# Second attention with row maxima by four head pairs instead of eight, and half of the shared expert moved into the routing

## The reference, cut to what matters

```python
# attention b: 16 heads of 8, per sample 256 queries x 256 keys
attn = jnp.einsum('abhqd,abhkd->abhqk', q, k) * scale
attn = jax.nn.softmax(attn, axis=-1)
out  = jnp.einsum('abhqk,bhkd->abhqd', attn, v)
out  = jnp.swapaxes(out, 1, 2).reshape(B, N, D)      # then @ proj_w.T + proj_b
# ffn: 64 experts of width 64, 8 chosen per token out of 4 of 8 groups, and a shared expert of width 128
h       = jax.nn.silu(g) * u * coef[:, :, None]
moe_out = jnp.einsum('tei,eih->th', h, Wd)
shared  = jax.nn.silu(x @ SWg) * (x @ SWu) @ SWd
```

## Time and profile before

| | us |
|---|---|
| median of 3 runs | 1084.95 (1084.47 to 1090.1) |
| the profiled execution's own time | 1086.67 |
| its span | 1084.9 |
| second attention's loop, from DVE's first uninterrupted maxima to the last copy of its output | 645.1 to 777.7 |
| from there to the first matmul of the shared expert's second half | 777.7 to 808.0 |
| expert loop of the second FFN and the end | 808.0 to 1084.9 |

### The profile page before, as it was taken

How to read it: one execution, slowest core, us unless ns; L and a number is a source line. 1 busy time by engine, 2 the same in 40 slices (tenths; PEclk the granted TensorE clock), 3 DMA queues, 4 the chain that set the end, 5 groups by cost and what they waited for, 6 DMA issues and landing times. The chain is left out here.

```text
span 1084.9 us, 17540 instructions
## 1 busy us (share of the span) xinstructions
PE 971.3 (90%) x5387; PEld 694.7 (64%) x5387; DVE 959.2 (88%) x1447; ACT 671.2 (62%) x848; POOL 368.7 (34%) x266
## 2 busy tenths in 40 slices
PE   6767887878669999999999899899889999999997
PEld 4533444444347888888888555455568888888886
DVE  7799999999988999999999797987589999999997
ACT  4779999999934545445445554876544544545544
POOL 2054666667901433333331211111203333333330
PEclk9865555555669999999999998999789999999999
DMA  2000000000119555555550000112049555555521
GB/s 59 1 1 1 1 1 1 1 1 1 52 30 215 157 160 151 147 157 147 155 153 4 1 1 1 23 23 31 16 107 225 151 147 157 148 154 155 147 85 39
DMA packets 50711, 86.94 MB, mean 80 GB/s; under 512 B 20092, under 2 KB 33404, under 8 KB 50556
## 3 DMA queue, kind: packets, MB, share of 16 engines
q1 hardware_dynamic: 50664, 86.34, 30.6%
HBM read 83.33 MB, written 2.98 MB: 80 GB/s over the span
## 5 line engine op out<-in xcount | busy, mean ns | idle before, releaser
L1514 ACT ACTIVATE sg<-ps 128x512 f32<-128x512 f32 x264 | 156.8, 594 | 264.8 <-PE ps L523 263.2
L523 PE MATMUL ps<-xh,whi 128*128 128x512 f32 x528 | 206.2, 391 | 1.3 <-ACT b L1330 1.3
L523 PE MATMUL ps<-xl,whi 128*128 128x512 f32 x528 | 205.9, 390 | 0.0
L523 PE MATMUL ps<-xh,wlo 128*128 128x512 f32 x528 | 205.8, 390 | 0.0
L2329 DVE TENSOR_TENSOR hf<-sg,ps 128x512 f32<-128x512 f32 x264 | 170.3, 684 | 29.9 <-DVE hl L2336 24.4
L1727 POOL CAST whi<-wraw 128x384 fp32r<-128x384 f32 x66 | 66.3, 1004 | 370.2 <-PE ps L523 285.5
L1647 POOL TENSOR_TENSOR rr<-xr,rr 128x2048 f32<-128x2048 f32 x32 | 145.2, 4569 | 125.0 <-ACT rr L1305 71.2
L2336 DVE TENSOR_TENSOR hl<-hf,hh 128x1024 fp32r<-128x1024 f32 x132 | 178.2, 1350 | 0.8 <-DVE hf L2329 0.8
L2341 DVE TENSOR_TENSOR hf<-hf,cbc 128x1024 f32<-128x1024 f32 x128 | 157.6, 1231 | 13.4
L1542 ACT ACTIVATE hh<-hf 128x1024 fp32r<-128x1024 f32 x132 | 139.2, 1055 | 4.6 <-DVE hf L2341 4.6
L1729 POOL TENSOR_TENSOR wlo<-wraw,whi 128x384 fp32r<-128x384 f32 x66 | 116.3, 1762 | 5.3
(11 more groups left out here) (277 smaller groups left out, 1512.3 us busy)
## 6 DMA issues: line engine op xcount, KB each, us to landing
cbc<-routing_coefficients SPq DMA_DIRECT2D x256, 256.0 KB, 3.8
wraw<-in_wexp_dram SPq DMA_DIRECT2D x66, 192.0 KB, 2.7
X<-in_x_dram SPq DMA_DIRECT2D x4, 256.0 KB, 4.8
routing_coefficients<-cT SPq DMA_DIRECT2D x8, 128.0 KB, 2.3
out_dram<-X SPq DMA_DIRECT2D x4, 256.0 KB, 2.9
heads_by_row<-o_all SPq DMA_DIRECT2D x12, 72.0 KB
b_rows<-heads_by_row SPq DMA_DIRECT2D x12, 72.0 KB, 2.7
rope_in<-in_consts_dram SPq DMA_DIRECT2D x1, 512.0 KB, 3.4
```

The source lines that it names most:

```text
L523: return pe.matmul(o, l, r, start=start, stop=stop, **kw)
L1514: act.activation(sg[c % 2][:, :], bank(4 + 2 * (c % 2)), ACT.Silu).then_inc(s_sg, 1)
```

## The change

The maxima are handled in *quads* of four units (`QUAD = UNITS // 2`), 16 rounds instead of 8, each with half as many maxima; the distance AHEAD falls from 11 to 8. The round's steps on PE stand at V % 4 = 1 and 2 instead of V % 8 = 0, 1 and 2. The path's steps stand some units earlier. `copy_out`'s last pair but one gets bank 2 beside bank 6. In the steps without raw scores, extra matmuls are put in (`TAIL_FILL`). The transposed tokens of the second FFN's groups 0 to 2 are copied by ACT instead of DVE, those of group 3 by DVE. The sigmoids of half 0 are taken group by group. The routing of half 0 is spread between the steps of the last two quarters of the path. In `prepare_f(1)` the shared expert's chunks 2 and 3 come on PE directly behind chunks 0 and 1, ahead of the second half's coefficients; DVE multiplies gate and up of chunks 0 and 1 between `route_masks` and `route_experts`. No product is left out in either version.

```diff
-AHEAD = UNITS + 3
+QUAD = UNITS // 2
+AHEAD = QUAD + 4
...
+        def pair_bank(n):
+            return 2 if n == 2 * B - 2 else 6
...
-            WAITS_FOR_PATH = {39: 4, 46: 3, 47: 4, 55: 4, 62: 3, 63: 4}
+            WAITS_FOR_PATH = {36: 4, 41: 3, 42: 4, 52: 4, 57: 3, 58: 4}
+            TAIL_FILL = {56: 1, 57: 1, 58: 2, 59: 1, 60: 2, 61: 1, 62: 2, 63: 2, 64: 2, 65: 2, 66: 2}
...
             def b_max_step(V):
-                s, at = (V - UNITS) // UNITS, (V - UNITS) % UNITS
-                if V >= UNITS and at == 0:
-                    b_max_transposed(s)
-                elif V >= UNITS and at in (1, 2):
-                    b_max_selected(s, at - 1)
+                k, at = V // QUAD - 1, V % QUAD
+                if 0 <= k < 2 * B:
+                    if at == 1:
+                        b_max_transposed(k)
+                    elif at == 2:
+                        b_max_selected(k)
...
                 for V in range(2, AHEAD):
                     b_tiles(-1, V)
                     b_max_step(V)
-                    if V >= AHEAD - 3:
-                        keep_busy(3, 6)
+                    keep_busy(3, 3)
...
+                    if U in (56, 57):
+                        pe.wait_ge(s_mx, 2 * B * UNITS + U - 57)
+                        logits(1, 0, U - 56)
...
             def prepare_f(f):          # PE
                 for c in range(2):
                     gate_up((PAIRS + 1) * FF_STEPS * f + c, 3, c, True)
+                if f == 1:
+                    shared_second(f)   # gate_up for chunks 2 and 3
...
             def samples_b():           # POOL
-                for s in range(B):
-                    max_split(s)
-                    if s == 1:
+                for k in range(2 * B):
+                    max_split(k)
+                    if k == 3:
                         pool.wait_ge(s_q2, 4)
                         pool.tensor_tensor(xb, xb, pb_s[:, :].unsqueeze(1).broadcast_to([P, TILES, P]), ALU.add
                                            ).then_inc(s_pbx, 1)
...
             def prepare_f(f):          # DVE
                 if f == 1:
-                    route_experts(f, 0)
+                    lows(f, 1)
                 route_bests(f, 1)
                 route_groups(f, 1)
                 route_masks(f, 1)
+                if f == 1:
+                    shared(f, 0)
                 route_experts(f, 1)
-                lows(f, 1)
+                if f == 0:
+                    lows(f, 1)
```

More of the change, by code:

```diff
@@ L952, in pv_b @@
                 if C % 2 == 0 and half == 0 and C >= 2:
-                    pe.wait_ge(s_bev, C // 2)
-                last = pv(vt, s, c, wr[:, C % CHUNKS, :], bank(6)[:, C % 2 * N:(C % 2 + 1) * N], (half,))
+                    if pair_bank(C // 2) == 2:
+                        pe.wait_ge(s_mx, 2 * B * UNITS - 2)
+                    else:
+                        pe.wait_ge(s_bev, min(C // 2, 2 * B - 2))
+                last = pv(vt, s, c, wr[:, C % CHUNKS, :], bank(pair_bank(C // 2))[:, C % 2 * N:(C % 2 + 1) * N], (half,))
                 if half == MT - 1:
@@ L1091, in gate_up, with shared_second @@
                     last.then_inc(done, 1)
+            def shared_second(f):
+                pe.wait_ge(s_xl, FF_STEPS * (f + 1))
+                for c in range(2, FF_STEPS):
+                    gate_up((PAIRS + 1) * FF_STEPS * f + c, 3, c, False)
             def prepare_f(f):
@@ L1133, in y @@
                     last.then_inc(s_yd, 1)
-                pe.wait_ge(s_xl, FF_STEPS * (f + 1))
-                for c in range(2, FF_STEPS):
-                    gate_up(s0 + c, 3, c, False)
+                if f == 0:
+                    shared_second(f)
                 with pe.Fori(0, PAIRS // 4) as i:
@@ L1429, in samples_b, with copy_xT, logit_exps @@
                         f_norm_rstd(1, 2)
-            def logit_exps(f, i):
-                act.wait_ge(s_lg, lap(f, i, 1))
+            def copy_xT(g, n):
+                act.wait_ge(s_fxnT, GROUPS + g + 1)
+                act.activation(f_xT[g][:, :], bank(n), ACT.Copy).then_inc(s_fxT, 1)
+                act.wait_ge(s_fxT, GROUPS + g + 1)
+                f_high(g)
+            def logit_exps(f, i, groups=range(2)):
+                act.wait_ge(s_lg, lap(f, i, groups[-1]))
                 if f == 0:
                     act.wait_ge(s_S, CHUNKS * B - 1)
-                for g in range(2):
-                    at = bank(spare(f, i, g) + 1) if f == 0 else bank(i)[:, g * GTILES * E:(g + 1) * GTILES * E]
+                for g in groups:
                     act.activation(route[f].sc[i][:, g * GTILES:(g + 1) * GTILES, :].rearrange("p t e -> p (t e)"),
-                                   at[:, 0:GTILES * E], ACT.Exp, scale=-1.0).then_inc(s_sc, 1)
+                                   logit_bank(f, i, g), ACT.Exp, scale=-1.0).then_inc(s_sc, 1)
             def o_transposed_b(c, n):
@@ L1514, in silu, with high, shared_second @@
                 act.activation(sg[c % 2][:, :], bank(4 + 2 * (c % 2)), ACT.Silu).then_inc(s_sg, 1)
+            def high(m, ring):
+                act.wait_ge(s_h, m + (1 + CR_H))
+                act.wait_ge(s_yd, m + (CR_YD - 3))
+                act.activation(hh[ring][:, :], hf[ring % 2][:, :], ACT.Copy).then_inc(s_hh, 1)
+            def shared_second(f):
+                s0 = (PAIRS + 1) * FF_STEPS * f
+                for c in range(2, FF_STEPS):
+                    silu(s0 + c, c, s0 + c - 1)
+                    if c == 2:
+                        high(FF_PAIRS * f, 2)
             def prepare_f(f):
@@ L1536, in experts @@
                 s0 = (PAIRS + 1) * FF_STEPS * f
-                def high(m, ring):
-                    act.wait_ge(s_h, m + (1 + CR_H))
-                    act.wait_ge(s_yd, m + (CR_YD - 3))
-                    act.activation(hh[ring][:, :], hf[ring % 2][:, :], ACT.Copy).then_inc(s_hh, 1)
                 p0 = FF_PAIRS * f
-                for c in range(2, FF_STEPS):
-                    silu(s0 + c, c, s0 + c - 1)
-                    if c == 2:
-                        high(p0, 2)
+                if f == 0:
+                    shared_second(f)
                 with act.Fori(0, PAIRS // 4) as i:
@@ L1895, in tiles, with sigmoids @@
                 step(last)
-            def sigmoids(f, i):
-                sc = route[f].sc[i]
-                dve.wait_ge(s_sc, lap(f, i, 1))
+            def sigmoids(f, i, g=None):
+                sc = route[f].sc[i] if g is None else route[f].sc[i][:, g * GTILES:(g + 1) * GTILES, :]
+                dve.wait_ge(s_sc, lap(f, i, 1 if g is None else g))
                 if f == 0:
@@ L2221, in head_max, with shift @@
                                           AX_X, ALU.max).then_inc(s_mx, 1)
-                def shift(s, half):
-                    dve.wait_ge(s_mq, 2 * s + half + 1)
+                def shift(k):
+                    s, half = k // 2, k % 2
+                    dve.wait_ge(s_mq, k + 1)
                     if s >= 2:
```

238 lines of the change are left out of this document (118 added, 120 removed).

## The result

| us | before | after |
|---|---|---|
| median | 1087.89 (1084.47 to 1090.1, 5 runs) | 1104.99 (1104.36 to 1115.04, 5 runs) |
| ratio, 95% interval | | 1.0169 [1.0141, 1.0198] |
| profiled execution, its span | 1086.67, 1084.9 | 1115.04, 1113.3 |
| first maximum / end of the last | 641.3 / 751.1 | 644.3 / 780.9 |
| last copy of the attention's output, its end | 777.7 | 805.5 |

I forecast 1072 (1064 to 1080). The kernel came out 33 us above that. The profiled execution of after is the longest of its five, 10 us above their median. A ratio leaves out executions that took over 1.5% longer than the fastest of the same kernel.

The account below looks back on a forecast made before the run. DVE was taken to bound the attention loop and the routing, PE the attention's end and the experts. Attention 11.2 us sooner plus routing 2.1 gave 13.3 off 1086.67, 1073.4; from the median 1071.6, predicted as 1072, range 1064 to 1080.

Parts of the forecast that it names:

- PE is shown busy for 82.83, but much of that is spaced by DVE's releases: Attention loop, 661.76 to 751.20: DVE is the bound, busy 79.05 of 89.44 us; PE's busy time is partly DVE's pacing.
- The addition to X: Loop, near V = 21: POOL's 4.57 us bias addition delays the next split; DVE idles 2.3 us, bounds 0 to 3.4.
- the tail's wait of 1.5: End of the attention, U = 60: PE waits 1.5 us (0 to 3) for DVE's normalised quarter 2.
- The rounds, 4.0: Loop: DVE's idle time at the present rounds, 4.0 of 10.4 us, goes; nothing charged for 8 added rounds.
- 6.4 forecast without the addition: Loop: DVE's remaining idle time, from extra matmuls ahead of scores in U < 12 and around the path, stays 6.4 us.
- The rival "slower": Loop: the round's chain isn't hidden, DVE waits 2.2 us in 14 rounds, 31 us more: 1103; chance 0.05.
- DVE waits ahead of the shifts: Loop: a sign named in advance that would show the prediction wrong; no size given.
- The start, 0.6: Ahead of the loop: DVE's idle time falls to 0.6 us from 4.5 in all, first round needing 8 maxima, not 16.
- The end of the attention, 20.2: From U = 56 without raw scores to the last output copy: 20.2 us at full clock, ending at 766.5 instead of 777.7.
- The rival "half clock in the tail": End of the attention: PE's clock falls behind its wait at U = 60, up to 6 us longer: 1078; chance 0.17.
- The routing, gain 2.1: From last attention copy to first expert: 12 matmuls moved away save 2.7 us, less 0.3 and 0.3, gain 2.1.

Follow-up runs that it names:

- f1: The changed kernel (lead 8) with POOL's addition to X in four pieces behind shifts 4 to 7 instead of one piece: 1092.8 us, 1.0047 to before.
- f2: The changed kernel with lead 9 instead of 8 and POOL's addition to X in four pieces: 1081.3 us, 0.9940 to before.
- e3: The kernel before with AHEAD 12 instead of 11, ACT's step of the round moved with it: 1096.9 us, 1.0084 to before.
- e1: The changed kernel with AHEAD 9 instead of 8, ACT's token copies one step earlier: 1086.6 us, 0.9981 to before.
- f3: The changed kernel (lead 8), addition left whole, with 12 extra matmuls on PE ahead of its wait for it: 1095.0 us, 1.0052 to before.
- f4: The changed kernel with lead 9, addition in four pieces, DVE's normalising of quarter 2 ahead of group 0's sigmoids: 1079.8 us, 0.9916 to before.
- g1: The changed kernel with lead 9, addition in four pieces, normalising first, one fill instead of two ahead of units 0 to 11: 1084.2 us, 0.9942 to before.

## Why the prediction was wrong, by its steps

- **"PE is shown busy for 82.83, but much of that is spaced by DVE's releases", and its unchanged cost per unit: the step that failed first.** I took AHEAD as a distance in time alone and a unit's matmuls at the price of before. The lead's parity decides whether raw and shifted scores run beside each other: 0.44 or 0.68 us a step, 13 us over the 56 steps that have both. Measured: 11 us at nearly the same mean clock (f1 to f2), 8 (before to e3), and 18 with a higher clock beside it (after to e1). With 0.68 and 0.57 for the value product, half a round's products and the fills, PE is later than DVE's 1.2 us a unit and bounds the loop.
- **The addition to X, "2.3 (0 to 3.4)": the second that failed.** The wait was sized rightly (2.72 on DVE). Its price was 12 us (f1), 10 of them by the clock (f3). I weighed the fall of the clock for the tail's wait of 1.5 and gave it 0.17 there, and did not ask the same of the longer wait in the loop. By the Trainium skill's rule on the swinging clock, which I had cited ("TensorE: Matmul & The Clock Gate", A second HAM failure mode: psum-queue depth-cycling), short idle times between groups of matmuls make the clock swing. The trace of after agrees for this wait, with 50 us at half behind 1.68; waits of 2.14 (f4) and 1.88 (f1) at the full clock were not followed by a fall.
- **The rounds, 4.0:** the waits are gone where I had them go, and 2.5 of the 4.0 show. In 661 to 751 f4 has 7.9 us of idle time ahead of the maxima, 10.4 before (6.4 forecast without the addition), and none at the rounds of 681 to 698. The rival "slower", 14 rounds of 2.2, is dead: e1, f2 and f4 have all 16 rounds and are no slower than before, and e3 loses 8 us with 8 rounds. "DVE waits ahead of the shifts" does come in after, 0.68 each, but at half clock only; of the loop's ten shifts at the full clock only the last waits, 0.36.
- **The start, 0.6:** held at the full clock. The sum counts from 645.1, behind a first wait of 1.0 that stands before too. Behind it f1 idles 0.4 us up to the first shift, g1 0.2, after 0.4. What I had not forecast is that this first wait grows with the clock at half: 2.3 in after (granted 0.66 to 0.77 from 641 to 647) and in f4, 1.0 in f1 and g1. Why the clock falls there I can't explain.
- **The end of the attention, 20.2 from V = 64 to the last copy:** 21.3 in f4, at the full clock. After has 24.6, because the wait at U = 60 (1.61, forecast 1.5) is followed by half clock from 792 to 799. The rival "half clock in the tail" held in this execution, at 3 of the 6 us that I gave it (24.6 against 21.3).

```profile
792.00 0.63 PE L1008 MATMUL ps<-cst,b_otok 128*128 128x128 f32 x4 [1.61 <-DVE b_otok L2280]
...
792.79 0.80 PE L539 MATMUL ps<-q,b_kt 32*128 32x256 f32 x4
```

- **The routing, gain 2.1:** the residual is 6.1 behind the last copy (forecast 6), the coefficients 23.9 behind it (22 to 23), the first expert 2.35 behind them (2.3). From last copy to first expert that is 32.3 instead of 33.0, so 0.7 of the 2.1 came; 1.2 are lost between the residual and the coefficients, where the route with its two products takes 14.05 (13.7 forecast) and its start waits 0.63 for ACT.

```profile
811.59 0.69 DVE L2298 TENSOR_TENSOR X<-X,ps 128x512 f32<-128x512 f32 x1 [0.71 <-PE ps L539]
...
821.41 0.69 DVE L1926 TENSOR_TENSOR sfc<-sc,eb_s 128x512 f32<-128x512 f32 x1 [0.63 <-ACT sc L1503]
834.77 0.69 DVE L1985 SCALAR_TENSOR_TENSOR coef<-wsel,wrec 128x512 f32<-128x512 f32 x1 [0.23 <-DVE wrec L1978]
```

The balance: 1072 + 11 for the lead's parity (f1 to f2) + 12 for the addition's wait (after to f1) is 1095, and 10 are left. With both mended f2 is at 1081.3, 9 above the forecast. A profiled execution was forecast at 1073.4; g1's is 1076.3, 2.9 above it, and its stages account for that: its maxima end 105.6 us behind the first (forecast 105.0, of which 2.3 are for the addition's wait, which g1 doesn't have), the tail has 21.2 (20.2), from last copy to first expert 32.2 (30.9). Without the 2.3 the loop, the tail and the routing are some 5 us longer than their terms. Of f2's 9 us the rest goes with the fills and a lower mean clock (0.872 in f2's median run, 0.879 in g1's) and isn't taken apart further. What stays open is why the clock falls near 640 in some of these kernels and not in others with the same matmuls around it, and why it fell behind f2's wait of 2.50 and not behind f4's of 2.14. No run tested the new places of the path's steps, the second bank of `copy_out` or `TAIL_FILL` by themselves.

## What to carry to other kernels

Where small matmuls of two streams are issued in turn, work out for both which rows of the array they use before changing the distance between them; a lead has a parity as well as a length. Price a wait on PE by what the clock does behind it, not by its own length, and cover one that can't be removed with matmuls that nobody reads. Split a long instruction of a helping engine so that each piece fits the gap that the new, shorter rounds leave.

## What the runs showed of the hardware that I had not expected

- Matmuls of 32 rows that take different rows of the array start within 0.01 us of each other; when both streams take the same rows their pairs follow each other, 0.24 us more for a group of eight at the full clock (0.44 to 0.68) and 0.42 at half (0.74 to 1.16). The Trainium skill says of the former that matmuls on distinct row groups run at once ("TensorE: Matmul & The Clock Gate", Part 3: Packing small matmuls — row/col tiling). The trace of before showed it already, in the starts of single matmuls.
- One wait of 1.7 us on PE was followed by 50 us at half clock, and with 12 matmuls in it whose result nobody reads the clock stayed at 1.00.
- DVE's subtraction of two SBUF tiles took 3.53 us instead of 0.68 beside an addition on POOL, while DVE's maxima from PSUM kept 1.29 for two beside the same addition.
